# Plain attention of a transformer block: heads multiplied in pairs on half arrays, maxima taken a pair at a time, and the next batch projected during the last quad

## The reference, cut to what matters

```
q = (src @ Wq + bq).reshape(B, T, N_HEAD, HEAD_DIM)
k = (src @ Wk + bk).reshape(B, T, N_HEAD, HEAD_DIM)
v = (src @ Wv + bv).reshape(B, T, N_HEAD, HEAD_DIM)
scores = jnp.einsum('bqhd,bkhd->bhqk', q, k) * scale
probs = jax.nn.softmax(scores, axis=-1)
attn = jnp.einsum('bhqk,bkhd->bqhd', probs, v).reshape(B, T, D_MODEL)
attn = attn @ Wo + bo
x = _layer_norm(src + attn, ln1_g, ln1_b)
```

## Time and profile before

| | us |
|---|---|
| median of 3 runs | 2310.1 (2309.88 to 2313.03) |
| the profiled execution, its own time | 2310.43 |
| its span | 2308.6 |
| PE busy in the span | 1958.1 (85%) |
| DVE busy | 1359.2 (59%) |
| ACT busy | 958.1 (42%) |
| POOL busy | 953.9 (41%) |
| mean granted clock of PE, share of full speed | 0.939 |

### The profile page before, as it was taken

The page is one execution under the profiler, slowest core; times in us unless marked ns, Lnnn a source line. Parts: engine busy times, 40 slices in busy tenths (PEclk is TensorE's granted clock), DMA queues, the critical chain, the costliest instruction groups (busy, mean ns, idle before and its releaser), DMA issues. The chain is left out here.

```text
span 2308.6 us, 37690 instructions
## 1 busy us (share of the span) xinstructions
PE 1958.1 (85%) x12145; PEld 1220.4 (53%) x12146; DVE 1359.2 (59%) x2919; ACT 958.1 (42%) x1361; POOL 953.9 (41%) x761
## 2 busy tenths in 40 slices
PE   6888988889888706999759998999989999898997
PEld 3454554545545305888635454655546455454654
DVE  4665766657666443667576565655546655465561
ACT  3655656556565412344214334142332424324142
POOL 4322130221302153344345637456373754638454
PEclk9999999999999857999969999999999999999999
DMA  6400000000000053555330010100101000010000
GB/s 205 156 9 0 9 9 0 9 0 9 9 0 1 0 211 123 198 206 183 115 85 1 1 38 1 38 1 1 38 1 38 1 10 29 1 38 1 17 12 10
DMA packets 56173, 104.81 MB, mean 45 GB/s; under 512 B 7238, under 2 KB 46566, under 8 KB 50156
## 3 DMA queue, kind: packets, MB, share of 16 engines
q1 hardware_dynamic: 52972, 94.71, 12.1%
q0 software_dynamic: 3072, 8.39, 1.1%
HBM read 76.35 MB, written 26.74 MB: 45 GB/s over the span
## 5 line engine op out<-in xcount | busy, mean ns | idle before, releaser
L368 POOL TENSOR_TENSOR a_probs<-a_probs 128x512 f32<-128x512 f32 x288 | 360.4, 1284 | 348.1 <-PE a_psO L686 347.1
L517 DVE CUSTOM_DVE_ANT_0 a_junk<-a_psM,a_alibi 128x512 bf16<-128x512 f32 x512 | 333.8, 689 | 236.1 <-PE a_psM L646 213.9
L1157 DVE TENSOR_REDUCE f_q_tok<-f_psR 128x1 f32<-128x512 f32 x512 | 336.4, 688 | 151.7 <-PE f_psR L1276 150.8
L451 ACT ACTIVATE a_probs<-a_psS 128x1024 f32<-128x1024 f32 x256 | 249.2, 1022 | 360.0 <-PE a_psS L672 270.5
L1118 ACT ACTIVATE f_probs<-f_psS 128x1024 f32<-128x1024 f32 x256 | 262.5, 1033 | 107.6 <-PE f_psS L1296 107.2
L1276 PE MATMUL f_psR<-f_kZ,f_qM 128*128 128x512 f32 x512 | 236.4, 491 | 39.4 <-DVE f_q_tok L1157 15.8
L686 PE MATMUL a_psO<-a_probs,a_v 128*32 128x512 f32 x2048 | 260.3, 631 | 0.0
L1000 POOL TENSOR_TENSOR f_oT<-f_oT,f_rsum 128x512 f32<-128x512 f32 x32 | 41.0, 1281 | 350.2 <-DVE f_rsum L1168 350.2
L1276 PEld LDWEIGHTS f_psR<-f_kZ,f_qM 128*128 128x128 f32 x512 | 101.1, 198 | 158.3 <-DVE f_q_tok L1157 94.7
L1296 PE MATMUL f_psS<-f_qS,f_kZ 128*128 128x512 f32 x512 | 177.2, 431 | 5.9 <-ACT f_probs L1118 5.2
L646 PE MATMUL a_psM<-a_kH,a_qH 64*128 64x512 f32 x512 | 129.7, 503 | 42.8 <-DVE a_n_tok L517 42.4
(11 more groups left out here) (199 smaller groups left out, 3880.8 us busy)
## 6 DMA issues: line engine op xcount, KB each, us to landing
w_w_high<-w_parts SPq DMA_DIRECT2D x19, 1024.0 KB, 5.4
w_w_low<-w_parts SPq DMA_DIRECT2D x19, 1024.0 KB, 7.4
sorted_x<-f_zeros SPq DMA_DIRECT2D x1, 4864.0 KB, 19.9
e_xs<-sorted_x SPq DMA_DIRECT2D x19, 256.0 KB, 2.7
sorted_z<-e_z SPq DMA_DIRECT2D x19, 256.0 KB, 2.2
f_xn<-in_L_attn_x SPq DMA_DIRECT2D x8, 512.0 KB, 3.5
f_w_raw<-in_L_ffn_W SPq DMA_DIRECT2D x4, 1024.0 KB, 9.2
w_parts<-f_w_high SPq DMA_DIRECT2D x4, 1024.0 KB, 3.9
```

Source lines behind the costliest of these rows:

```text
L368: nc.gpsimd.tensor_tensor(slot, slot, probs[:, GRP * (j - 1) + e, :], ALU.add).then_inc(added.sem, 1)
L451: nc.scalar.activation(probs[:, slots, :], psS[:, 2 * p:2 * p + 2, :], ACT.Exp).then_inc(exp_done.sem, 1)
L517: nc.vector.tensor_tensor_reduce(out=junk[:, a, :], in0=psM[:, a, :], in1=alibi[:, h, :], scale=1.0, scalar=-3.0e38, op0=ALU.add, op1=ALU.max,
L1157: nc.vector.tensor_reduce(q_tok[:, c, h, NEG:NEG + 1], psR[:, bank_of("max", m), :], AX.X, ALU.max, negate=True).then_inc(max_done.sem, 1)
```

## The change

- **Pairs.** `kZ` (eight zero-padded tiles) becomes `kP` (one tile for each of the eight pairs, all 128 rows used), and `qM` grows from two tiles to four. A product for the maxima is now a pair of heads: two matmuls of 64 rows, one in each half of the array, into the two banks of `psM`. There are 32 of them for a batch, and each is reduced by one DVE instruction over both banks.
- **Banks.** `psR` (three banks in turn) is replaced by `psM` (two banks, for the maxima and, in the last quad, for rows and projection) and `psT` (one). Keys, queries and shifted queries of the quads go to `psT` or to bank 0 of `psS`.
- **Periods.** A period is one tile of 128 keys for all four heads of a quad: an early maxima product, the scores of both pairs, a late maxima product, the transposes, then `weigh` of the period before. `multiply_for_max(m)` waits for `max_done` of m - 1, for `psM` holds only one product.
- **Order around the batch.** Ten of the 32 products (`AHEAD = 2` past the first quad's eight) stand in `prepare`, between them the output in four pieces of four. Rows are turned and projected in the periods of the last quad. `prepare` begins behind them.
- **Other engines.** ACT makes one copy of keys for a pair in place of two. POOL applies `norm1` in place of DVE, in `finish_rows`; the split of W1 is divided between the first and the last batch.

```
+    QP = 2
+    MQ = QP * TT
+    AHEAD = 2
+    PREPARE = [("keys", 0), ("queries", 0), ("keys", 1), ("queries", 1), ("max", 0), ("keys", 2), ("max", 1),
+               ("queries", 2), ("out", 4), ("max", 2), ("out", 4), ("keys", 3), ("max", 3), ("queries", 3), ("out", 4),
+               ("max", 4), ("shifted", 0), ("out", 4), ("max", 5), ("max", 6), ("max", 7), ("max", 8),
+               ("shifted", 1), ("max", 9)]
+    def side(quad, j):
+        items = [[], [("shifted", 2 * quad + 2), ("keys", 2 * quad + 4)],
+                 [("queries", 2 * quad + 4), ("keys", 2 * quad + 5)],
+                 [("shifted", 2 * quad + 3), ("queries", 2 * quad + 5)]][j]
+        return [(kind, n) for kind, n in items if n < PAIRS]
+    def maxima(quad, j):
+        first = MQ * (quad + 1) + 2 * j + AHEAD
+        return [m if m < QUADS * MQ else None for m in (first, first + 1)]
...
-        psR = ps("psR", [P, RING, S])
+        psM = ps("psM", [P, 2, S])
+        psT = ps("psT", [P, S])
...
             def take_max(b, m):
-                h, c = divmod(m, TT)
+                pair, c = divmod(m, TT)
                 dve.wait_ge(max_ps.sem, max_ps.at(b, m))
-                nc.vector.tensor_reduce(q_tok[:, c, h, NEG:NEG + 1], psR[:, bank_of("max", m), :], AX.X, ALU.max,
+                nc.vector.tensor_reduce(q_tok[:, c, 2 * pair:2 * pair + 2, NEG], psM[:, :, :], AX.X, ALU.max,
...
+            def quads(b, more, before=None):
+                for r in range(PERIODS):
+                    quad, j = divmod(r, TT)
+                    for m in maxima(quad, j):
+                        if m is not None:
+                            take_max(b, m)
+                    if (quad, j) == (0, 0) and before is not None:
+                        dve.wait_ge(r1_done.sem, r1_done.at(before, 1))
+                        norm1.statistics(dve, before, r1)
+                    if (quad, j) == (1, 2) and more:
+                        dve.wait_ge(x_in.sem, x_in.at(b + 1, 0))
+                        norm0.statistics(dve, b + 1, xn)
+                    if (quad, j) == (QUADS - 2, TT - 1) and more:
+                        norm0.apply(dve, b + 1, xn, xn, xn_done)
+                    if quad and j == 1:
+                        invert_sums(b, quad - 1)
+                    if quad == QUADS - 1 and more and j in (1, 2):
+                        for n in (2 * j - 2, 2 * j - 1):
+                            add_bias(b + 1, n)
+            def turn(b, more):
+                for n in (TT, TT + 1):
+                    add_bias(b + 1, n)
+                invert_sums(b, QUADS - 1)
+                prepare(b + 1, b)
+                quads(b + 1, more, b)
...
+            def multiply_for_max(b, m):
+                pair, c = divmod(m, TT)
+                if m == 0:
+                    pe.wait_ge(bias_done.sem, bias_done.at(b, NB - 1))
+                else:
+                    pe.wait_ge(max_done.sem, max_done.at(b, m - 1))
                 if c == 0:
+                    pe.wait_ge(kP_done.sem, kP_done.at(b, pair))
+                    pe.wait_ge(qM_done.sem, qM_done.at(b, pair))
+                for a, half in enumerate(HALVES):
+                    last = nc.tensor.matmul(psM[:, a, :], qM[half, pair % 4, c * P:(c + 1) * P], kP[half, pair, :],
+                                            start=True, stop=True, tile_position=(FB * a, 0))
+                last.then_inc(max_ps.sem, 1)
...
             def batch(b, more):
+                for r in range(PERIODS):
+                    quad, j = divmod(r, TT)
+                    items = side(quad, j)
+                    early, late = maxima(quad, j)
+                    rows = more and quad == QUADS - 1
+                    if early is not None:
+                        multiply_for_max(b, early)
+                    for p in range(QP):
+                        scores(b, r, p, taken[p])
+                    if late is not None:
+                        multiply_for_max(b, late)
+                    taken = [dict(items[:-1]), {}]
+                    if items:
+                        turn_free(b, *items[-1])
+                        transpose_pair(b, *items[-1])
+                    for kind, n in items[:-1]:
+                        pe.wait_ge(exp_done.sem, exp_done.at(b, QP * r))
+                        transpose_pair(b, kind, n)
+                    if rows and j == 0:
+                        transpose_rows(b + 1)
+                    if r:
+                        weigh(b, *divmod(r - 1, TT))
+                    if rows and j:
+                        for n in (2 * j - 2, 2 * j - 1):
+                            project(b + 1, n)
```

More of the change, by code:

```diff
@@ L1048, in batch, with quads @@
                 nc.gpsimd.tensor_tensor(x1_b, x1_b, offset, ALU.add).then_inc(x1_done.sem, 1)
-            passes(pool, batch)
+            norm0.raise_variance(pool, 0)
+            reset_maxima(0)
+            pool.wait_ge(loads, LOADS)
+            for t in range(TT):
+                low_parts(0, t)
+            def quads(b, more, before=None, splits=()):
+                xnb_sum(b)
+                if before is not None:
+                    finish_rows(before)
+                for e in splits[0:1]:
+                    split_w1(e)
+                normalize(b, 0)
+                if more:
+                    norm0.raise_variance(pool, b + 1)
+                for e in splits[1:]:
+                    split_w1(e)
+                normalize(b, 1)
+                if more:
+                    reset_maxima(b + 1)
+                normalize(b, 2)
+                if more:
+                    for t in range(TT):
+                        low_parts(b + 1, t)
+                normalize(b, 3)
+            quads(0, True, splits=range(EARLY))
+            with pool.Fori(0, B - 2) as b:
+                quads(b + 1, True, b)
+            quads(B - 1, False, B - 2, splits=range(EARLY, NE))
+            finish_rows(B - 1)
         @block.scalar
@@ L1110, in batch, with exponentials @@
[L1110 to L1126 removed]
+            def exponentials(b, r, p):
+                act.wait_ge(score_ps.sem, score_ps.at(b, QP * r + p))
+                if p == 0:
+                    act.wait_ge(pv_done.sem, pv_done.at(b, r - 2))
+                nc.scalar.activation(probs[:, r % 2, 2 * p:2 * p + 2, :], psS[:, 2 * p:2 * p + 2, :],
+                                     ACT.Exp).then_inc(exp_done.sem, 1)
@@ new lines, in prepare @@
+            def prepare(b):
+                for kind, n in PREPARE:
+                    if kind in take:
+                        take[kind](b, n)
+            def batch(b, more):
+                for r in range(PERIODS):
+                    quad, j = divmod(r, TT)
+                    rows = more and quad == QUADS - 1
+                    exponentials(b, r, 0)
+                    if rows and j > 1:
+                        high_parts(b + 1, 2 * j - 3)
+                    exponentials(b, r, 1)
+                    for kind, n in side(quad, j):
+                        take[kind](b, n)
+                    if rows and j == 0:
+                        take_xnT(b + 1)
+                    if rows and j in (1, 2):
+                        high_parts(b + 1, 2 * j - 2)
+                    if j == 0 and quad:
+                        take_output(b, quad - 1)
@@ L1129, in batch @@
                     prepare(b + 1)
+            take_xnT(0)
+            for t in range(TT):
+                high_parts(0, t)
             prepare(0)
@@ L1279, in shifted @@
[L1279 to L1297 removed]
+                    last = nc.tensor.transpose(bank[:, t * P:(t + 1) * P], heads, idn[:, :])
@@ new lines, in scores @@
+            def scores(b, r, p, taken):
+                quad, j = divmod(r, TT)
+                pair = QP * quad + p
+                needs = dict(taken)
+                if j == 0:
+                    needs["shifted"] = max(pair, needs.get("shifted", 0))
+                if r > 0:
+                    pe.wait_ge(exp_done.sem, exp_done.at(b, QP * (r - 1) + p))
+                for kind, n in needs.items():
+                    pe.wait_ge(reader[kind].sem, reader[kind].at(b, n))
+                for a, half in enumerate(HALVES):
+                    last = nc.tensor.matmul(psS[:, 2 * p + a, :], kP[half, pair, j * P:(j + 1) * P],
+                                            qS[half, pair % 4, :], start=True, stop=True, tile_position=(FB * a, 0))
@@ L1376, in batch @@
                         project_output(b, n, False)
+            transpose_rows(0)
+            for n in range(NB):
+                project(0, n)
             prepare(0)
```

363 lines of the change are left out of this document (144 added, 219 removed).

## The result

The changed kernel takes 2334.18 us (median; 2331.05 to 2334.94), the kernel before 2309.99 in the same session: ratio 1.0102, 95% interval 1.0085 to 1.012. It is 1.0% slower, 24 us. The forecast was 2329, in a range of 2300 to 2358.

The account below looks back on a forecast made before the run. Plain attention was taken as bound by the product-reduction-product chain, with PE full in quad 3 and part of the preparation. Terms 6.3 + 3.3 + 6 x 2.2 - 5.1 + 1.0 = +18.7, rounded to +19, on 2310.4 gave 2329 us, range 2300 to 2358.

Parts of the forecast that it names:

- the likeliest case: Whole kernel: links bare, clock low once a turn; 2314 to 2342 us, chance 0.47.
- The link: Maxima product to reduction to next product: 0.53 + 1.22 + 0.05 = 1.80 us, 32 in a batch.
- The rotary hand-over: Rival on product to reduction: 0.78 in place of 0.53 in nearly all 256 links, +60 us, 2390; chance 0.07.
- Periods: Quads 0 to 2: a period takes 4.25 us with two transpose groups, 3.82 with one, 3.60 with none.
- Detours: DVE's statistics and inversions behind late reductions in the quads stick out by 1.3, 0.4, 0.7 and 0.9 us.
- Quad 3: Last quad with projection, PE full: 20.4 us against 25.8 before, 5.4 gained.
- Preparation: From the end of the last weighing, ending in four bare links: 24.7 us against 17.7, 7.0 lost.
- The clock: End of preparation into quad 0: thin chain drops PE's granted clock to 0.50; +4 us a turn, bounds 2.7 and 7.
- a rival with a chance of 0.18: Quads: the clock falls again in one or two more periods a turn, +2.4 us each; 2347 to 2367; chance 0.18.
- The rival that the clock costs nothing: End of preparation: clock level holds, so 2296 us, faster; chance 0.20, including the other way to a gain.
- The ends: Start of batch 0 +6.3 us, first turn +3.3, last batch -5.1.
- The tail: End of the last batch: POOL applies norm1, four instructions at 0.73 us or less; +1.

Follow-up runs that it names:

- The first experiment: Changed kernel with the reduction over both banks cut into one per bank, each with its own signal: 2288.1 us, 0.9902 of before.
- third experiment: Changed kernel with 22 matmuls that nobody reads added per batch in PE's idle time, in the preparation and first period: 2311.8 us, 1.0007 of before.
- The fourth experiment: Changed kernel with the next batch's rows transposed and projected behind quad 3's last weighing, not during it: 2349.2 us, 1.0166 of before.
- second: Changed kernel with the sixteen output pieces in twos behind products 1 to 8 of the preparation, not fours behind 1 to 4: 2293.9 us, 0.9929 of before.
- sixth experiments: Changed kernel with a reduction per bank, output pieces spread in twos, and the last batch's norm1 applied by DVE: 2257.3 us, 0.978 of before.

## Why the prediction was right

Time, sign and mechanism were those of the likeliest case. By its steps, forecast and measured:

- *The link* 1.80: 1.82. Its reduction of 1.22: 1.222, though the slope was drawn through an addition of 256 elements and not through a second reduction, so this close a hit owes something to luck. The rotary hand-over played no part. The first experiment, which changes only the link, moved the time by 46 us. The Trainium skill (TensorEngine Tiling (Array Packing), PSUM Bottleneck) says that packing doesn't speed up the emptying of PSUM; the trace agrees, with 1.22 of 1.82 in the reduction. Of the 16 us a turn that I estimated from the same page's speedup (Theoretical Speedup), the quads gained 0.8.
- *Periods* 4.25, 3.82, 3.60: 4.27, 3.84 and 3.65.
- *Detours* of DVE: for the inversions 0.4 and 0.9, measured 0.31 and 0.74; for the statistics 0.7 and 1.3, measured 0.55 and 0.87. All a little smaller; the 0.87 stands in a stretch of low clock, and at full clock, in the third experiment, the same detour shows 1.18.
- *Quads 0 to 2* 49.0, and some 3 for the clock in them: 51.6.
- *Quad 3* 20.4: 20.4. That it was 5.4 shorter than before is right as well, but I put this down to "the ends of DVE, ACT and POOL chains that stood bare around the projection". The fourth experiment divides it: 2.7 by the overlap, 2.05 because quad 3 alone takes 10.05 in place of 12.1, and 0.7 because rows and projection take 13.04 in place of 13.7.
- *Preparation* 24.7, and 0.8 for the clock: 25.25 in one turn, 26.95 in another, which met a short second stretch of low clock that I had not foreseen.
- *A turn at full clock* 94.1: 93.9 and 94.3, in the third experiment. *The clock* +4: 3.6 to 3.95 by the same turns. It is the term that decides the sign: 94.1 was under the kernel before, 98.1 over it. The forecast stretch came as told, once a turn, from product 8 to the third period. But by itself it costs some 3: the four turns that have no other take 96.7 to 97.2. The rest is the second short drops, which the prediction had left to a rival with a chance of 0.18, so that the mean of 4 is in part luck. The row that it leaned on, was also less bare than it said: in that stretch four transposes stand behind three of the five products, and PE is busy 6.69 of 10 us. The rival that the clock costs nothing had a chance of 0.20, and the filled kernel, at the time of before, is nearly its case.
- *A turn* 98.1, 2.2 more than before: 97.9 and 1.75 more, since the turn of the kernel before that I took as base, 95.87, is a little under the mean of its six.
- *The ends*: start +6.3, measured 55.36 - 49.78 = 5.6; first turn +3.3, measured 97.61 - 93.04 = 4.6; last batch 61.6, measured from 740.20 to 801.13, 60.9. The kernel before took 784.7 - 719.54 = 65.2 there and not 66.7, so that this term is -4.3 and not -5.1.
- *The tail* +1: this term was mis-sized, by 2.7. I gave POOL 0.73 an instruction, by the nearest instruction of POOL in the earlier trace rows, and it takes 1.22; with the hand-overs +3.7 (6.28 from the power to the product with the gain, 2.61 before).
- *The other phases* "as they were": they brought 3 more. The cause is not shown; a lower mean clock it is not.

The sum of the plain attention was 18.7 and came to 20. That it came so near is in part errors that cancel: six turns were put at 13.2 and came to 10.5, and the start came 0.7 cheaper, while the first turn, the last batch and the tail came 1.3, 0.8 and 2.7 dearer. The 3 us of the phases behind it make most of the 5 us between 2329 and 2334.

## What to carry over

Here pairing halved PE's work for these products, but if the pair fills all banks of its kind, product and reader alternate, and the loop runs at the sum of both; count that sum before counting the halved work. Where such a chain can't be avoided, spread independent work over all its links and not over the first ones: the same sixteen matmuls in another order were worth 30 us in the traced execution and 40 by the median, and together with a signal for each bank and the last norm on DVE they made the kernel 2.2% faster than before instead of 1.0% slower. Read the granted clock beside each thin chain: here it cost more a turn (3.6 to 3.95) than the change lost (1.75).

## What the runs showed of the hardware

- POOL's subtraction and multiplication with a mean and a scale per row, 128x256 f32, takes 1.22 us; DVE does four of the same in 1.38 us, 345 ns each.
- One 64x512 product on half the array holds PE for 0.42 us when it stands between other matmuls, two on both halves 0.43.
- DVE's reduction of 1024 elements over two banks takes 1.22, two of 512 take 1.29 together: cutting it cost 0.07.
- Filling PE's idle time with matmuls that nobody reads made the whole program 22 us shorter. Why the clock falls in the first period even where the chain ahead of it was filled with real work (second and sixth experiments), and why some turns of the filled kernel lose it and others not, stays open.
